# Joined high and low products in one contiguous 512-column run: a layout change in the down projection, and the same joining for probabilities times values

## The reference, cut to what matters

```python
def attn(x):                                   # x: [8, 1024, 256], one head of 256
    q, k, v = split(x @ w_qkv.T)
    probs = softmax((q @ k.T) * 0.25)
    return (probs @ v) @ w_proj.T + b_proj     # after a swap of axes and a reshape
def ffn(h):                                    # 8192 tokens, 16 experts, 1024 tokens each
    scores = softmax(h @ gate_w.T).T
    w, idx = top_k(scores, 1024)
    eo = (gelu(h[idx] @ Wg) * (h[idx] @ Wu)) @ Wd * w
    return scatter_add(eo) + (gelu(h @ Sg.T) * (h @ Su.T)) @ Sd.T
x = x + layernorm(attn(layernorm(x)))
x = x + layernorm(ffn(layernorm(x)))
```

## Time and profile before

| what | value |
|---|---|
| median of 3 runs | 2100.78 us (2098.29 to 2102.92) |
| the profiled execution | 2095.7 us, span 2093.9 us |
| PE busy | 2022.8 us, 97% of the span |
| DVE, ACT, POOL busy | 1254.0, 968.9, 440.0 us |
| granted TensorE clock, mean | 0.986 |
| PV matmuls (256 columns), whole run | 1536, groups with means of 283 to 295 ns |
| L1246 (512 columns, two runs of 256) | 1024, mean 398 ns |
| L1248 (256 columns) | 1024, mean 281 ns |

### The profile page before, as it was taken

How to read it: one execution, slowest core, us unless ns; L and a number is a source line. 1 busy time by engine, 2 the same in 40 slices (tenths; PEclk the granted TensorE clock), 3 DMA queues, 4 the chain that set the end, 5 groups by cost and what they waited for, 6 DMA issues and landing times.

```text
span 2093.9 us, 31249 instructions
## 1 busy us (share of the span) xinstructions
PE 2022.8 (97%) x11802; PEld 1759.3 (84%) x11802; DVE 1254.0 (60%) x2655; ACT 968.9 (46%) x1802; POOL 440.0 (21%) x449
## 2 busy tenths in 40 slices
PE   7999999999994999999999999999999999999996
PEld 6899999999993888888888888888888888888885
DVE  5686686586664887565556555545454545444565
ACT  4464564574552434443434343434353444444443
POOL 0000000000001000124222422342224232331255
PEclk9999999999995999999999999999999999999998
DMA  3011110110014211233333333333333333333266
GB/s 113 1 41 42 61 63 41 60 61 41 41 63 151 93 61 61 86 99 63 82 72 74 78 75 79 75 80 77 78 92 62 92 65 88 82 75 98 56 198 130
DMA packets 55615, 159.82 MB, mean 76 GB/s; under 512 B 9536, under 2 KB 26048, under 8 KB 48320
## 3 DMA queue, kind: packets, MB, share of 16 engines
q1 hardware_dynamic: 28976, 116.16, 15.3%
q0 software_dynamic: 26512, 41.96, 12.6%
HBM read 98.78 MB, written 59.31 MB: 76 GB/s over the span
## 4 chain that ended last, share of the span: by engine, by line
PE 64%; DVE 2%; POOL 1%; DMA 1%; ACT 0%; issue 0%; DVEq 0%; SPq 0%; POOLq 0%; ACTq 0%
PE mo_psD L1246 11%; PE mo_psG L58 7%; PE mo_psU L58 7%; PE mo_psG L60 7%; PE mo_psG L59 7%; PE mo_psU L60 7%; PE mo_psU L59 7%; PE mo_psD L1248 6%; PE mo_psD L58 1%; PE mo_psX L1172 1%; PE mo_psD L59 1%; PE mo_psD L60 1%; PE mo_psX L987 1%; DMA mo_F<-ACC 0%; DVE mo_st L1469 0%
## 5 line engine op out<-in xcount | busy, mean ns | idle before, releaser
L1505 DVE TENSOR_TENSOR mo_HF<-mo_psU,mo_HF 128x512 f32<-128x512 f32 x320 | 221.2, 691 | 353.2 <-ACT mo_HF L1345 353.0
L1345 ACT ACTIVATE mo_HF<-mo_psG 128x512 f32<-128x512 f32 x320 | 191.7, 599 | 478.3 <-PE mo_psU L60 474.4
L1246 PE MATMUL mo_psD<-mo_wd,mo_H_hi 128*128 128x512 f32 x1024 | 362.7, 398 | 0.0
L1740 POOL DMA_INDIRECT ACC<-mo_OUT,mo_GI x128 | 202.9, 1585 | 670.4 <-DVE mo_OUT L1582 662.5
L1248 PE MATMUL mo_psD<-mo_wd,mo_H_lo 128*128 128x256 f32 x1024 | 287.5, 281 | 0.0
L1246 PEld LDWEIGHTS mo_psD<-mo_wd,mo_H_hi 128*128 128x128 f32 x1024 | 192.4, 188 | 47.5
L1450 DVE TENSOR_TENSOR mo_H_lo<-mo_HF,mo_H_hi 128x512 fp32r<-128x512 f32 x300 | 204.8, 683 | 0.0
L1323 ACT ACTIVATE mo_H_hi<-mo_HF 128x512 fp32r<-128x512 f32 x320 | 199.7, 624 | 1.0 <-DVE mo_HF L1505 1.0
L1248 PEld LDWEIGHTS mo_psD<-mo_wd,mo_H_lo 128*128 128x128 f32 x1024 | 193.4, 189 | 1.2
L1582 DVE SCALAR_TENSOR_TENSOR mo_OUT<-mo_psD,mo_TW,mo_OUT 128x256 f32<-128x256 f32 x128 | 61.9, 484 | 215.6 <-ACT mo_OUT L1412 215.6
L1412 ACT ACTIVATE mo_OUT<-mo_psD,mo_TW 128x256 f32<-128x256 f32 x128 | 60.9, 476 | 268.8 <-PE mo_psD L1248 268.8
(11 more groups left out here) (254 smaller groups left out, 5053.1 us busy)
## 6 DMA issues: line engine op xcount, KB each, us to landing
X1a<-wg_in SPq DMA_DIRECT2D x16, 1024.0 KB, 5.0
X1a<-wu_in SPq DMA_DIRECT2D x16, 1024.0 KB, 4.9
X1a<-wd_in SPq DMA_DIRECT2D x16, 1024.0 KB, 4.9
XN<-XNB SPq DMA_DIRECT2D x8, 1088.0 KB, 4.1
X<-x_in SPq DMA_DIRECT2D x8, 1024.0 KB, 6.3
out_dram<-X SPq DMA_DIRECT2D x8, 1024.0 KB, 4.3
XN2T<-xn2T SPq DMA_DIRECT2D x8, 1024.0 KB, 3.8
mo_F<-ACC SPq DMA_DIRECT2D x7, 1024.0 KB, 13.5
```

The lines of the kernel that those rows point to most:

```text
L1246: pe.matmul(psD[:, t % 2, :].rearrange("p (z d) -> p z d", z=2), h_hi, wd_both[:, :, it, :], start=(it == 0), stop=False)
L1345: a.activation(HF[:, it % 2, :], psG[:, it % 2, :], ACT.Gelu).then_inc(s_gelu, 1)
L1505: v.tensor_tensor(HF[:, it % 2, :], psU[:, it % 2, :], HF[:, it % 2, :], ALU.mult).then_inc(s_mul, 1)
L1740: g.indirect_dma_start(out=io["ACC"], out_offset=bass.IndirectOffsetOnAxis(ap=GI[n % 2][:, 4 * tb + t:4 * tb + t + 1], axis=0), in_=OUT[:, ...
```

## The change

It has two parts. The down weights are laid out as [slice][high, low][256], so that the 512 columns of L1246 are one contiguous run; the number of matmuls, their sizes and what is written are as before. The high and low halves of the weights are made by the same instructions, which write two runs of 256 instead of one of 512.

For PV the same joining is new. The values are laid out as [t][high, low][256], and each block t takes two matmuls instead of three: one of 512 columns into both halves of `psO` or `psL`, and one of 256 columns for the low probabilities. The output is the sum of the two halves of the bank, so DVE gets a new instruction at the head of step s: a sum of the two halves of tile s-3 (`tensor_reduce` over pairs of elements that lie 256 columns apart) into a new SBUF tile `Osum`. `O_hi` and `O_lo` read `Osum` instead of PSUM. `O_hi` of a tile moves from the end of ACT's step s-2 to the head of step s-3, so ACT has a step 10 as well, and PE's wait before it reuses a bank is for the sum (s_os) and not for `O_lo`.

```diff
-        V = pair("V", [P, NT, D])
+        V_both = sb("V", [P, NT, 2, D], F32R)
+        V = [V_both[:, :, z, :] for z in (0, 1)]
+        Osum = sb("Osum", [P, 2, D])
...
         def output_bank(i):
-            return (psO, psL)[i % 2][:, 0:D]
+            return (psO, psL)[i % 2]
...
-                                wait(pe, s_ol, 8 * r + i2 - 1)
+                                wait(pe, s_os, 8 * r + i2 - 1)
...
-                                i = mm3(pe, output_bank(i2), PT[0][:, i2 % 2, t, :], PT[1][:, i2 % 2, t, :],
-                                        V[0][:, t, :], V[1][:, t, :], t == 0, t == NT - 1)
+                                pe.matmul(output_bank(i2)[:, :], PT[0][:, i2 % 2, t, :], V_both[:, t, :, :].rearrange("p z d -> p (z d)"),
+                                          start=(t == 0), stop=False)
+                                i = pe.matmul(output_bank(i2)[:, 0:D], PT[1][:, i2 % 2, t, :], V[0][:, t, :], start=False, stop=(t == NT - 1))
...
-                    for step in range(NT + 2):
-                        i0, i1, i2 = step, step - 1, step - 2
-                        if R.ln_next and step >= NT:
+                    for step in range(NT + 3):
+                        i0, i1, i3 = step, step - 1, step - 3
+                        if i3 >= 0:
+                            if i3 == 0:
+                                wait(a, s_y, 4 * r)
+                            wait(a, s_ri, 8 * r + i3 + 1)
+                            wait(a, s_os, 8 * r + i3 + 1)
+                            a.activation(O[0][:, i3, :], Osum[:, i3 % 2, :], ACT.Copy, scale=rinv[:, i3:i3 + 1]).then_inc(s_oh, 1)
+                        if R.ln_next and NT <= step < NT + 2:
...
-                        if i2 >= 0:
-                            if i2 == 0:
-                                wait(a, s_y, 4 * r)
-                            wait(a, s_ri, 8 * r + i2 + 1)
-                            wait(a, s_pv, 8 * r + i2 + 1)
-                            a.activation(O[0][:, i2, :], output_bank(i2), ACT.Copy, scale=rinv[:, i2:i2 + 1]).then_inc(s_oh, 1)
...
+                    if i3 >= 0:
+                        wait(v, s_pv, 8 * r + i3 + 1)
+                        v.tensor_reduce(Osum[:, i3 % 2, :], output_bank(i3)[:, :].rearrange("p (z d) -> p d z", z=2), AX.X,
+                                        ALU.add).then_inc(s_os, 1)
...
-                        v.scalar_tensor_tensor(O[1][:, i3, :], output_bank(i3), rinv[:, i3:i3 + 1], O[0][:, i3, :].bitcast(F32),
+                        v.scalar_tensor_tensor(O[1][:, i3, :], Osum[:, i3 % 2, :], rinv[:, i3:i3 + 1], O[0][:, i3, :].bitcast(F32),
...
-        t = self.new(n, [s[0], 2] + s[1:], F32R)
+        t = self.new(n, [s[0], s[1], 2, s[2]], F32R)
...
-        wd = [wd_both[:, z, :, :] for z in (0, 1)]
+        wd = [wd_both[:, :, z, :] for z in (0, 1)]
...
-                            pe.matmul(psD[:, t % 2, :].rearrange("p (z d) -> p z d", z=2), h_hi, wd_both[:, :, it, :],
+                            pe.matmul(psD[:, t % 2, :], h_hi, wd_both[:, it, :, :].rearrange("p z d -> p (z d)"),
```

More of the change, by code:

```diff
@@ L200, in attention @@
         s_t, s_pth, s_ptl = sem("s_t"), sem("s_pth"), sem("s_ptl")
-        s_pv, s_oh, s_ol = sem("s_pv"), sem("s_oh"), sem("s_ol")
+        s_pv, s_os, s_oh, s_ol = sem("s_pv"), sem("s_os"), sem("s_oh"), sem("s_ol")
         s_r1, s_xn, s_ry, s_yn, s_x1, s_r2, s_xn2 = (sem(n) for n in ("s_r1", "s_xn", "s_ry", "s_yn", "s_x1", "s_r2", "s_xn2"))
```

## The result

The changed kernel takes 2128.4 us (2127.71 to 2130.77, 4 runs) where the kernel before took 2101.35 in the same comparison (2098.29 to 2102.92, 4 runs): ratio 1.0133, 95% interval 1.0115 to 1.015, 27 us slower. The prediction was 2131 us, with 2106 to 2156 as its range. The profiled execution took 2130.77 us, its span is 2129.0; for the kernel before these were 2095.7 and 2093.9.

What follows compares the result with a forecast made beforehand. PE was taken as the bound, with almost no slack in DVE. Six round boundaries of 5.1 us plus 3 for the others, less 3 on PV, gave +31 us on the median of 2100.78: 2131 us, range 2106 to 2156.

Steps and rivals of the forecast that it cites:

- The down projection, 0: Expert part: the contiguous layout changes nothing, since the surcharge belongs to alternating 512 and 256 columns; 0 us.
- rival 4: Down projection and PV: the break makes the pair dear, contiguous pairs take 0.340 us, 23 us gained before boundaries; chance 0.09.
- PV on PE, 3 us: Attention part on PE: each joined PV saves 0.06 us, 64 times 3.8 us, taken as 3 us.
- The sum, 0.69 us: New DVE instruction: reading 512 PSUM elements takes 0.69 us, with 1.11 kept for the range.
- DVE late by 1.2 us without the block: Middle of a round: four sums, 2.44 us, less DVE's idle 0.20 + 1.01, leave it 1.2 us late at step 7.
- POOL's block, 2.3 us a round, and 0.3 on O_lo: Each round: DVE's step 4 chain meets POOL's add and loses 2.3 us; O_lo can lose up to 0.3 in step 3.
- Rival 2: POOL's block does not come or unseen slack covers part: +15 us, from +5 to +20; chance 0.16.
- The round's end, 5.1 us a boundary: Chain from PV(7) to W at a round's end: DVE's lateness delays W from 470.27 to 475.4, 5.1 us a boundary.
- The sum.: Total: six boundaries of 5.1 plus 3 make 34 us lost, less 3 on PV: +31 us.
- Boundary 0 to 1: First round boundary, without the tasks: two sums in its chain and some waiting, an estimate of 2 us.
- rival 1: Dearer sum of 1.11 us (+52), or PE's clock falling in waits at the boundary (+46); +42 to +60, chance 0.27.

Runs made afterwards that it cites:

- e1: The kernel before with only the experts' down weights laid out contiguously, high then low per block: 2097.35 us against 2097.05, ratio 0.9995.
- e3: The kernel before with PV joined on PE only, no sum of the halves, so part of the output is missing: 2093.27 us against 2097.05.
- e10: e3 with O_lo made over 16 of its 256 columns in all rounds but the first: 2086.38 us against 2096.07, ratio 0.9957.
- e12: e5 with POOL's second add held back as in e2: 2100.67 us against 2097.24 for the kernel before, ratio 1.0015.
- e4: The changed kernel with each sum issued twice, the first into a spare tensor nobody reads: 2158.3 us, ratio 1.029.
- e5: e3 with the sum added on DVE from step 3 on, read by nobody: 2113.16 us against 2097.74 for the kernel before, ratio 1.007.
- e2: The changed kernel with POOL's second add held until DVE has done the next batch's norm statistics: 2115.62 us against 2097.05 before, ratio 1.0086.
- e8: e2 with the sum and O_lo moved behind PT_lo on DVE, and O_hi behind the exponential on ACT: 2157.22 us, ratio 1.0278.
- e9: e2 with each O_lo one step later behind the maximum, the sum behind PT_lo, and O_hi after the normalizations: 2128.54 us, ratio 1.0157.
- e11: e2 with joined PV and its sum only for products 0 to 2, three matmuls a block for the rest: 2096.13 us against 2097.24, ratio 0.9994.
- e7: e2 with O_lo moved off DVE: ACT scales the sum, then rounds it to O_hi, and POOL subtracts: 2133.38 us, ratio 1.0167.

## Why the prediction was right

**The down projection, 0.** Right: e1 shows it alone. With it rival 4 falls.

**PV on PE, 3 us.** The duration was right and a bit low: PV to S is 0.10 us shorter in a middle step, estimated 0.06. e3 gives 4 us as a whole. What I had not said is where: the middle rounds return it as a wait for DVE's `PT_lo`. In the kernel before DVE is ready 0.30 us ahead of PV(7) (463.96 + 1.27 against 465.53). In e3, with PE earlier, the chain meets POOL's add in every round, and DVE comes later than before. e10, in which it does so once and DVE has less to do, shows PE's saving whole.

**The sum, 0.69 us.** Right, 0.68. The Trainium skill, PSUM — Partial Sum Buffer, Specifications, speaks of matmuls that a non-contiguous pattern slows; carried over to DVE's read at a step of 1 KB it would have given more, and this trace doesn't bear that out.

**DVE late by 1.2 us without the block.** Right in mechanism. In e12, where the load stands alone, it makes 1.7 us over PE's own time and 1.1 over the kernel before; e4 shows that the dose after the slack is used up costs its full 8 x 0.60 us.

**POOL's block, 2.3 us a round, and 0.3 on O_lo.** The 2.3 is right, and shown by taking it away: e12 against the rounds of e5 at full clock gives 2.3 us a round, and e2 against after 1.3, with 0.75 moved to `O_lo`. The 0.3 is wrong: in the six rounds with the chain `O_lo` keeps its 0.48 us. I also priced the block as new in all six rounds, though the earlier trace rows show it in one of them in the kernel before, and it was there in two: those two grew by 3.6 and 4.3 us, the other four by 4.7 to 5.2. Rival 2, that it would not come, falls, but its price for a kernel without the block, 2.5 us a boundary and +15 us, is near what e2 shows: 79.75 - 76.49 = 3.26 us and +19. What I undervalued is `O_lo` as a victim once the add is held back.

**The round's end, 5.1 us a boundary.** The sizes held, one place did not. PV(7) was to start 3.92 us later; added up over the distances of PE's starts it is 3.5. W was to be 5.1 later, less the 0.4 a round that I took off for PV, and is 81.23 - 76.49 = 4.7. But PE does not run undisturbed up to PV(7): it stops 0.7 us before T(5) already and 2.05 more before the first half of PV(6). I had reckoned with 4 us of slack between `PT_lo` and its PV and used the distance of middle steps for it. In step 8 PV(6) has no S ahead of it, so it comes sooner; and I had left out the transposes, which wait for DVE as well. All of these are one lateness of DVE seen at successive places: PV(6) and PV(7) both wait for `PT_lo`. So the sum was hardly touched by it.

**The sum.** Boundary 0 to 1 costs 1.9 us (2 estimated), the one after it 3.6, the next five 4.7 on average, the last nothing (1 estimated), and the stretch from the last W to the experts is 0.8 shorter. That is 28.4 us against the 31 predicted; the medians of all runs show 27. That it comes so close has some luck in it: the 0.3 on `O_lo`, the block counted as new in two rounds that had it, and 1 us for the last boundary were too much, while the clock, which I had left to rival 1, added a little.

**Rival 1.** No dearer sum. The clock does fall inside rounds, to 1.2 GHz for 3.4 us, but only twice (at 320.7 and 402.6 us of the trace), and the two rounds are 0.2 and 0.5 us longer than the others. That is far from the 2 to 3 us in each round of that rival. Its mechanism is real all the same: with more waiting it comes in every round (e4, e8), and costs 0.9 us in a round of e5 and 1.1 to 1.8 in one of e9.

## What to carry to other kernels

A kernel whose busiest engine is at 97% may still gain little from relieving it: look how closely the next engine keeps up with it in the stretch in question (here DVE is ready 0.30 us ahead of PV(7)), and pay attention to what the change hands to that engine. Price an added instruction as dose minus slack: against the kernel before, a round with 3 sums is 0.2 us longer (e11) and one with 8 sums 1.1 (e12), while 8 more on top of the changed kernel cost their full 4.8. And an instruction of an idle engine can be the dearest of all if it blocks: the smallest of these edits, e3, put a 0.17 us instruction behind POOL's add in every round. That took at most 0.6 us a round in e3, by the traces of e3 and e10, and 2.3 us where the sums had used up the slack (e5 against e12).

## What the runs showed of the hardware

- The expert part has the same code and data in all kernels, but for the layout of the down weights, and yet its profiled length went from 1418.7 us (e10) over 1422.0 (before) and 1425.6 (e1) to 1428.7 (after), without relation to the edit. In the longer ones PE pauses at places some 71 us apart, between two matmuls that wait for nothing in the trace. PE of the kernel after:

```profile
1001.70 0.39 PE L58 MATMUL mo_psU<-mo_XT_hi,wu_hi 128*128 128x512 f32 x1
1002.41 0.39 PE L59 MATMUL mo_psU<-mo_XT_lo,wu_hi 128*128 128x512 f32 x1 [0.32 <-issue]
```

  The start comes 0.71 us behind the one before in place of 0.23. The kernel after has six such pauses between 1002 and 1360 us, 3.0 us together, less than half of its 6.7; the kernel before has none. That they are fetches of instructions is a guess that I did not try. The spread makes a single profile uncertain by some 5 us to either side, which is why the comparison uses rounds and repeated runs.
- A matmul of 512 and one of 256 columns in alternation take 0.353 us a pair in the experts, contiguous or not, and (447.36 - 445.62)/5 = 0.348 in the attention part.
- A DVE reduction over pairs 1 KB apart in PSUM costs 0.68 us for 512 elements, as much as the plain `tensor_tensor` over 512 of the earlier trace rows, 0.69.
- A DVE instruction with two inputs in SBUF that starts behind the start of a POOL add of 2.4 us ends with the add or up to 0.3 us behind it (0.17 us instructions took 2.2 to 2.4). `O_lo` with one input in PSUM kept its 0.48 us beside such an add in e12; with both in SBUF it took 1.23 in e2 and 1.78 in e9.
- TensorE's granted clock fell to 1.2 GHz for 3.4 us or more behind PE's waits in a round. In e9 the matmuls of W, of 256 columns, start 0.21 us apart in such a stretch and 0.12 otherwise.
- POOL's subtraction of 256 elements a partition takes 0.74 us (e7), DVE's scaled one 0.48.
